# Gated cross-attention with a quantised feed-forward: the batch's row sum moves from TensorE to ScalarE and Pool, W1 is applied to the attended rows, and x is normalised on VectorE

## The reference

```python
h   = layernorm(x)
Sim = (h @ w1)[:, :, None] + (ctx @ w2)[:, None, :] + einsum('bid,bjd->bij', h * w3, ctx) + b_sim
A   = softmax(Sim, axis=2);            hq = einsum('bij,bjd->bid', A, ctx)
Bt  = softmax(max(Sim, axis=2), 1);    hc = einsum('bi,bid->bd', Bt, h)[:, None, :]
x   = x + tanh(g_xattn) * (concat([h, hq, h * hq, h * hc]) @ W_qv + b_qv)
x   = x + tanh(g_ffn) * ffn(layernorm(x))     # 256 -> 768 -> 256, weights and activations quantised
```

## Time and profile before

| | |
|---|---|
| median of 3 runs | 500.15 us (500.15 to 500.7) |
| the profiled execution | 500.24 us, its span 498.0 us |
| attention part | 0 to 224.7 us of the span |
| busy over the span | TensorE 467.1 us (94%), VectorE 347.6 (70%), ScalarE 278.5 (56%), Pool 42.8 (9%) |
| mean granted TensorE clock | 0.983 |

### The profile page before, as it was taken

How to read it: one execution, slowest core, us unless ns; L and a number is a source line. 1 busy time by engine, 2 the same in 40 slices (tenths; PEclk the granted TensorE clock), 3 DMA queues, 4 the chain that set the end, 5 groups by cost and what they waited for, 6 DMA issues and landing times.

```text
span 498.0 us, 6971 instructions
## 1 busy us (share of the span) xinstructions
PE 467.1 (94%) x2542; PEld 306.2 (61%) x2542; DVE 347.6 (70%) x648; ACT 278.5 (56%) x325; POOL 42.8 (9%) x51
## 2 busy tenths in 40 slices
PE   4899999998999979989999999999949999999997
PEld 3787885987488548754444444444414444588886
DVE  6464683687257754769443558999988888898874
ACT  3795241634151200528334379999977677888760
POOL 1111111242013110210000000000100000000000
PEclk9999999998999998999999999999969999999999
DMA  8920000200020020020000000000000000234432
GB/s 246 327 91 1 0 2 12 74 1 1 0 86 0 1 84 2 0 86 0 0 0 0 0 0 0 0 0 1 1 0 0 0 0 0 85 107 128 144 113 103
DMA packets 20671, 21.11 MB, mean 42 GB/s; under 512 B 826, under 2 KB 20393, under 8 KB 20649
## 3 DMA queue, kind: packets, MB, share of 16 engines
q1 hardware_dynamic: 20628, 20.82, 13.2%
q10 hardware_dynamic: 20, 0.00, 0.0%
HBM read 12.43 MB, written 8.39 MB: 42 GB/s over the span
## 4 chain that ended last, share of the span: by engine, by line
PE 56%; issue 17%; DVE 14%; ACT 10%; POOL 1%; DMA 1%; ACTq 0%; POOLq 0%; DVEq 0%
PE ps L672 11%; PE ps L647 10%; PE ps L652 5%; PE ps L495 4%; PE ps L491 4%; PE ps L474 4%; PE ps L499 4%; ACT ag L863 3%; PE ps L537 3%; ACT hid L870 3%; PE ps L454 3%; DVE hid L1279 2%; ACT gq L858 2%; PE ps L440 1%; PE ps L463 1%
## 5 line engine op out<-in xcount | busy, mean ns | idle before, releaser
L647 PE MATMUL ps<-xh,wuh 128*128 128x512 f16 x192 | 73.9, 385 | 9.3 <-DVE gq L1304 7.4
L647 PE MATMUL ps<-xh,wul 128*128 128x512 f16 x192 | 73.8, 384 | 0.0
L652 PE MATMUL ps<-xl,wuh 128*128 128x512 f16 x192 | 58.0, 384 | 0.0
L1251 DVE TENSOR_REDUCE cols<-hid x12 | 27.4, 2286 | 30.5 <-ACT hid L852 30.5
L852 ACT ACTIVATE hid<-ps 128x2048 f32 x12 | 22.5, 1875 | 34.5 <-PE ps L652 34.5
L647 PEld LDWEIGHTS ps<-xh,wuh 128*128 x192 | 19.0, 99 | 34.7 <-issue 11.2
L672 PE MATMUL ps<-wdh,oh 128*128 128x256 f16 x168 | 37.4, 273 | 0.0
L672 PE MATMUL ps<-wdl,oh 128*128 128x256 f16 x168 | 37.4, 273 | 0.0
L647 PE MATMUL ps<-xh,wgh 128*128 128x512 f16 x96 | 36.4, 379 | 0.7 <-DVE xh L1239 0.7
L647 PE MATMUL ps<-xh,wgl 128*128 128x512 f16 x96 | 36.4, 379 | 0.0
L491 PE MATMUL ps<-cw,aT 77*128 77x256 f32 x128 | 35.5, 392 | 0.9 <-ACT cols L801 0.9
(11 more groups left out here) (199 smaller groups left out, 945.9 us busy)
## 6 DMA issues: line engine op xcount, KB each, us to landing
x_scratch<-xa SPq DMA_DIRECT2D x4, 1024.0 KB, 4.4
xo<-x_scratch SPq DMA_DIRECT2D x16, 256.0 KB, 2.7
out_dram<-xo SPq DMA_DIRECT2D x15, 256.0 KB, 2.2
xa<-in_x SPq DMA_DIRECT2D x3, 1024.0 KB, 12.1
xa<-in_x SPq DMA_DIRECT2D x4, 256.0 KB, 4.7
wv<-in_L_xattn_W_qv SPq DMA_DIRECT2D x1, 1024.0 KB, 8.1
wr<-in_L_ffn_w_gate SPq DMA_DIRECT2D x1, 768.0 KB, 9.6
wr<-in_L_ffn_w_up SPq DMA_DIRECT2D x1, 768.0 KB, 11.0
```

The lines of the kernel that those rows point to most:

```text
L647: pe.matmul(ps[hf][:, q, :], w_[:, d, ds(k * P, P)], xh[:, d, n], start=d == 0 and w_ is wh, stop=False)
L652: mm = pe.matmul(ps[hf][:, q, :], wh[:, d, ds(k * P, P)], xl[:, d, n], start=False, stop=d == KD - 1)
L1251: dve.tensor_reduce(gmx[:, ds(k * 2 + hf, 1)], unit(hid, k, hf), AX.X, ALU.max, apply_absolute_value=True).then_inc(gm_done, 1)
```

## The change

What it does, part by part:

- **Attended x W1.** `context_w` and `context_wv` are gone. ScalarE copies `hq_bank` to SBUF (`hqT`), and `project` multiplies `hqT` by W1 itself. VectorE's `attended` reads `hqT` instead of `hq_bank`, so it waits for ScalarE. The bias is multiplied once by tanh(g) (`txb`) and added to `xa` by Pool (`bias_x`).
- **Row sums.** `row_sum` and `row_copy` are gone. ScalarE and Pool each weigh four of the eight row tiles of h in place (`row_weigh`, slot s = 1), and Pool adds them down to one tile (slots s = 1 and 2). `batch_cols` sums that tile over its partitions by a matmul.
- **The batch column one slot later.** `batch_cols` and `summary` move from s = 2 to s = 3, on TensorE right ahead of the `project` that needs `we`.
- **The norm of x** moves from ScalarE to VectorE; `row_shift` is gone.
- **Pool's order**: `y_std`, then `row_weigh` or `row_add`, then `row_std`, `bias_x`, and the weights.

```diff
@@ Pool
+            def row_weigh(b):
+                par = b % 2
+                pool.wait_ge(eb_rdy, b + 1)
+                for t in range(TB // 2, TB):
+                    i_ = pool.tensor_scalar(h[:, par, t, :], h[:, par, t, :], eb[:, t:t + 1], 1.0, ALU.mult, ALU.mult)
+                i_.then_inc(hp_rdy, 1)
+                pool.wait_ge(hp_rdy, b + 1)
+                pool.tensor_tensor(h[:, par, 4:6, :], h[:, par, 4:6, :], h[:, par, 6:8, :], ALU.add).then_inc(hsum_rdy, 1)
+            def row_add(b):
+                par = b % 2
+                pool.wait_ge(ha_rdy, b + 1)
+                pool.tensor_tensor(h[:, par, 0:2, :], h[:, par, 0:2, :], h[:, par, 2:4, :], ALU.add).then_inc(hsum_rdy, 1)
+                pool.wait_ge(hsum_rdy, 3 * b + 2)
+                pool.tensor_tensor(h[:, par, 0:2, :], h[:, par, 0:2, :], h[:, par, 4:6, :], ALU.add).then_inc(hsum_rdy, 1)
+                pool.wait_ge(hsum_rdy, 3 * b + 3)
+                pool.tensor_tensor(h[:, par, 0, :], h[:, par, 0, :], h[:, par, 1, :], ALU.add).then_inc(hs_rdy, 1)
+            def bias_x(n):
+                pool.wait_ge(h_rdy, n + 1)
+                if n == 0:
+                    pool.wait_ge(txb_rdy, 1)
+                x_ = xa[:, 2 * n:2 * n + 2, :]
+                pool.tensor_tensor(x_, x_, txb[:].unsqueeze(1).broadcast_to([P, 2, D]), ALU.add).then_inc(xb_rdy, 1)
...
                 if LAG <= m < L + LAG:
                     y_std(m - LAG)
+                b, s = m // NP, m % NP
+                if s == 1 and 1 <= b <= B:
+                    row_weigh(b - 1)
+                if s == 2 and 1 <= b <= B:
+                    row_add(b - 1)
                 if 1 <= m and m + 3 < N:
                     row_std(m + 3)
+                if s in (0, 3) and 4 <= m < N + 4:
+                    for n in range(2):
+                        bias_x(m - 4 + n if s == 0 else m - 5 + n)
@@ TensorE
             def attend(n):
-                ge(pe, pr_rdy, n)
+                ge(pe, hqT_rdy, n)
...
-            def project(n, summed=None):
+            def project(n):
...
-                    for k in range(2):
-                        pe.matmul(o_, aT[0:JP, par, k, q], cw[0:JP, b % 3, k, :], start=k == 0, stop=False)
-                        if summed is not None:
-                            row_sum(summed, 4 * t + k)
+                    for d in range(KD):
+                        pe.matmul(o_, hqT[:, par, d, q], wv[:, KD + d, :], start=d == 0, stop=False)
...
             def batch_cols(b):
-                pe.wait_ge(hrow_rdy, b + 1)
+                pe.wait_ge(hs_rdy, b + 1)
                 for d in range(KD):
-                    pe.matmul(m_bank[:, HC + d:HC + d + 1], hrow[0:1, d * P:(d + 1) * P], ones[0:1, 0:1], start=True, stop=True)
+                    pe.matmul(m_bank[:, HC + d:HC + d + 1], h[:, b % 2, 0, d * P:(d + 1) * P], ones[:, 0:1], start=True, stop=True)
...
                 if s == 3 and b + 1 < B:
                     context_bias(b + 1)
-                if m == 1:
-                    context_w(0)
-                if s == 0 and 1 <= b < B:
-                    context_w(b)
+                if s == 3 and 1 <= b <= B:
+                    batch_cols(b - 1)
                 if LAG <= m and late:
                     project(m - LAG)
@@ ScalarE
+            def attended(n):
+                act.wait_ge(hq_ps, n + 1)
                 ge(act, f_ps, n - 2 * NP + 1)
+                act.activation(hqT[:, par, :, s * PT:(s + 1) * PT], hq_bank.rearrange("p (d n) -> p d n", d=KD),
+                               ACT.Copy).then_inc(hqT_rdy, 1)
+            def row_weigh(b):
+                act.wait_ge(eb_rdy, b + 1)
+                for t in range(TB // 2):
+                    a_ = act.activation(h[:, b % 2, t, :], h[:, b % 2, t, :], ACT.Copy, scale=eb[:, t:t + 1])
+                a_.then_inc(ha_rdy, 1)
...
-                if m + 1 < N:
-                    norm_x(m + 1)
...
                     normed(m - 1)
                 if s == 1 and b == 1:
                     batch_exp(b - 1)
+                if 3 <= m <= N + 2:
+                    attended(m - 3)
+                if s == 1 and 1 <= b <= B:
+                    row_weigh(b - 1)
@@ VectorE
+            def norm_x(n):
                 dve.wait_ge(rstd_rdy, n + 1)
+                ge(dve, hc_ps, b - 1)
+                for t in range(2 * s, 2 * s + 2):
+                    c = par * TB + t
+                    i_ = dve.tensor_scalar(h[:, par, t, :], xa[:, b * TB + t, :], mv[:, par, t, 0:1], rstd[:, c:c + 1],
+                                           ALU.subtract, ALU.mult)
+                i_.then_inc(h_rdy, 1)
...
             def attended(n):
-                dve.wait_ge(hq_ps, n + 1)
+                dve.wait_ge(hqT_rdy, n + 1)
...
-                dve.tensor_tensor(prT[:, par, :, q], hq_bank.rearrange("p (d n) -> p d n", d=KD), hT[:, par, :, q],
-                                  ALU.mult).then_inc(pr_rdy, 1)
+                dve.tensor_tensor(prT[:, par, :, q], hqT[:, par, :, q], hT[:, par, :, q], ALU.mult).then_inc(pr_rdy, 1)
...
             def residual(n):
                 dve.wait_ge(f_ps, n + 1)
+                dve.wait_ge(xb_rdy, n + 1)
...
                 if m == 0:
-                    row_shift(3)
+                    norm_x(3)
+                if 3 < m and m + 1 < N and s < 3:
+                    norm_x(m + 1)
...
-                if 2 <= m and m + 2 < N:
-                    row_shift(m + 2)
-                if s == 2 and 1 < b <= B:
-                    summary(b - 1)
...
                 if 3 <= m <= N + 2:
                     attended(m - 3)
+                if s == 3 and 1 <= b <= B:
+                    summary(b - 1)
+                if s == 3 and m + 1 < N:
+                    norm_x(m + 1)
                 if LAG <= m and late:
                     residual(m - LAG)
                     norm_x1(m - LAG)
```

More of the change, by code:

```diff
@@ L586, in _ @@
                 if LAG <= m and not late:
-                    project(m - LAG, b - 1 if s == 2 and 1 <= b <= B else None)
+                    project(m - LAG)
                 if s == 1 and 1 <= b <= B and LAG <= m:
@@ L597, in _ @@
                     score(m - 1)
-                if s == 2 and b == 1:
-                    pe.wait_ge(eb_rdy, b)
-                    for t in range(TB):
-                        row_sum(b - 1, t)
                 if 2 <= m <= N + 1:
@@ L605, in _ @@
                     batch_max(b - 1)
-                if s == 2 and 1 < b <= B:
-                    batch_cols(b - 1)
                 if 3 <= m <= N + 2:
                     attend(m - 3)
-                if s == 2 and b == 1:
-                    batch_cols(b - 1)
                 if LAG < m:
@@ L1034, in last_y @@
             def last_y():
+                dve.wait_ge(xb_rdy, N)
                 for t in range(2):
@@ L1145, in _ @@
             stats(1)
-            row_shift(0)
+            norm_x(0)
             dve.wait_ge(bs_rdy, 1)
```

102 lines of the change are left out of this document (30 added, 72 removed).

## The result

The changed kernel takes 515.51 us (median of 4 runs, 514.09 to 516.36) against 500.15: ratio 1.0305, 95% interval 1.0277 to 1.0334. Its profiled execution took 514.09 us, its span 512.3. (Ratios leave out disturbed runs, one of e17's four and five of e18's ten; medians and the bounds beside them don't.) TensorE is busy for 461.2 us (90%), VectorE 366.4 (72%), ScalarE 277.4 (54%), Pool 91.3 (18%); the granted clock is 0.937 where it was 0.983.

A forecast was written before the change was run, and what follows sets the result against it. By time alone TensorE bounds the attention part, but the change lengthens VectorE's in-order waits. Walk -9.9, locks +8 and clock +4.8 sum to +2.9 us on a profiled 500.24 (median 500.15): forecast 503, range 493 to 511.

The forecast's parts named there:

- the slower side: Whole kernel: the chance that the changed kernel is slower, 0.51, against faster 0.36 and same 0.13.
- the walk: VectorE's slots between the starts of project(0), (4), (8), (12): +1.9, -1.7, -5.6, -4.5, sum -9.9 us.
- to project(0): Start up to project(0): VectorE and ScalarE alone form the chain, start moves from 48.17 to 50.0 to 50.1, +1.9 us.
- the lock term: Pool's added SBUF operations holding up VectorE's: 3, 2 and 3 us by stretch, +8; 0 at best, some 15 at worst.
- the price of bias_x: Pool's bias additions, four a batch at 1.05 us each, in front of the next slot's vp2; priced within +8.
- The clock: TensorE stands 4 us before each project(4b), then runs at half clock: three new losses, +4.8 us (0 to 6.4).
- The product, +1.4: VectorE's prT waits for ScalarE's copy, starting 1.5 us after the reciprocal instead of 0.1; nothing can fill it.
- The summary as a dead end: Slots with s = 3: prT, then summary, 1.35 us, and only then may project(4b) start.
- TensorE's loss of 27 us: TensorE's work removed: row sums 20.2 us and context_w 6.9, so its busy time falls by some 27 us.
- The lock rule: A Pool operation on SBUF shuts out some of VectorE's until it ends; prT with two SBUF inputs joins those.
- Pool's queue becomes the bound: Rival: y_std late in each slot 1 and 2 by 1 to 2 us over the forecast, 509 to 516; chance 0.10.
- The chain is relieved: Rival, faster: Pool's locks fall into VectorE's waits and the clock holds at short stands, 496 us; chance 0.31.

The follow-up runs named there:

- e17: Changed kernel with VectorE's product read from PSUM (hq_bank), ScalarE's copy behind it, and without bias_x: 489.02 us, ratio 0.9760.
- e18: Changed kernel with product from PSUM, sums as TensorE column matmuls, column and summary at s = 2, norm of x back on ScalarE: 501.57 us.
- e1: Changed kernel without Pool's 16 bias additions (bias left out of the result): 503.40 us, ratio 1.0064 to the kernel before.
- e3: Changed kernel with VectorE's product read from PSUM again and ScalarE's copy behind it: 500.46 us, ratio 1.0007 to the kernel before.
- e9: Kernel before the change with only batch_cols and summary moved to s = 3: 510.02 us against 500.64, ratio 1.0201.
- e10: Kernel before with batch vector by one-column TensorE matmuls, those of batches 0 to 2 two behind each W1 and W2 matmul: 498.97 us.
- e12: Changed kernel with product from PSUM, sums as TensorE column matmuls spread over attend, column and summary at s = 2, no bias_x: 489.09 us.

## Why the prediction was wrong

It gave the slower side 0.51, so naming the direction was close to a toss; it named the chain, and forecast 503 where 515.5 came: the sum was +2.9, the result +15.4 (+14 against the profiled execution). By its steps, in the profiled execution:

| stretch | forecast by the walk | after | over | e1 (no bias), over |
|---|---|---|---|---|
| to project(0) | 50.1 | 50.1 | 0.0 | +0.2 |
| (0) to (4) | 45.3 | 50.2 | +4.9 | +3.6 |
| (4) to (8) | 45.4 | 53.1 | +7.7 | +4.6 |
| (8) to (12) | 36.7 | 44.6 | +7.9 | +3.4 |
| (12) to the end | 310.7 | 314.2 | +3.5 | +0.7 |
| sum | 488.2 | 512.3 | +24.1 | +12.5 |

Over the walk the forecast booked 12.8 us, 8 for locks and 4.8 for the clock. Without the bias the excess is 12.5. So **the step that failed is the lock term, +8, and in it the price of bias_x**, which took 12.1 us by itself:

- *Its place.* The prediction had it "in front of the next slot's vp2", and gave the place right behind y_std to row_add. At 63.55 it met vp2 and cost it 0.5 us, as that has it. This holds only while row_std stands between y_std and bias_x, and it does so only in slots with m + 3 < N. In the slots 15, 16 and 19 bias_x came right behind y_std, where norm_x1 starts: at 163.57 and 208.07, though Pool had been idle for 16.91 and 10.82 us before y_std, two additions ran back to back and norm_x1 took 2.62 us instead of 0.74; at 172.99 `diag` took 1.40 and norm_x1 1.69. At 115.43 it pushed weight_n back, and this shows a way that the prediction did not price: Pool comes late first, and then VectorE waits for it:
```profile
115.43 2.50 POOL L414 TENSOR_TENSOR xa<-xa,txb 128x512 f32<-128x512 f32 x2
117.90 2.76 POOL L386 TENSOR_TENSOR wr<-wr,wsc 128x1536 f32<-128x1536 f32 x1
120.63 0.69 POOL L367 TENSOR_TENSOR cols<-cols 128x2 f32<-128x2 f32 x1
```
```profile
117.61 0.35 DVE L1033 TENSOR_SCALAR cols<-cols 128x2 f32<-128x2 f32 x1
...
118.66 2.09 DVE L1075 TENSOR_SCALAR diag<-ident,cols 128x128 f32<-128x128 f32 x1
```

  vp2 was there at 117.96, y_std started at 120.63, and `diag` took 2.09 us instead of 0.29. Not all of this is the bias: weight_n holds this slot in the other kernels too, at vp2. From the start of residual to that of norm_x1 it is 5.59 us here, 4.45 in e1 and 5.09 before. norm_x1 took over 2.2 us five times in all, two of them against bias_x and three against row_add.
- *Its length.* 512 columns were interpolated at 1.05 us; they took 1.27 (weighing one tile took 0.478, near the 0.45 taken).
- *Its sum.* "As the nearest row shows a full hit, I take 3 us ..., 2 ..., and 3": 8 us for 16 additions of bias, 16 weighings and 16 additions of rows. Removing the bias alone gave 12.1 us, more than the whole term; removing the sums alone gave 9.0. Less the clock (below, 6.9 to 10.4), 14 to 17 of the 24.1 us are left for this term, about the 15 that I had called every one in full.
- *What a hit costs.* 8.4 us on VectorE came with 12 us of time. A hit lengthens TensorE's stand too, and the half clock after it. The prediction added locks and clock as if one didn't feed the other.

**The clock**: +4.8 was taken for three new stands of 1.6. project(0), (4), (8) and (12) took 7.1, 8.3, 7.3 and 7.2 us instead of 5.3, 8.5 too much in all (29.9 - 4 x 5.35), of which before paid 1.6 at project(12): 6.9 new. The attends before project(4) and (8), 3.66 and 3.62 us instead of 1.89, were at half clock too, 3.5 more. Filling the stands gave back 7.4, though project(0) itself then starts 2.4 us later and project(12) stays at half clock. The term was short by at least 2.1. Its picture was off as well: no stand of 4 us lies before project(4) and (8), but one of 3.04 and 1.95 us at the scores and a second of 1.48, and the clock was down before the second began.

**After project(12)** the walk had no change, and that was wrong by 3.5 us. Without the bias it is 0.7: again bias_x, whose pairs reach 209 us.

**What held.** To project(0): 50.14, forecast 50.1; 5.98 us of it are the exchange, as e3 starts at 44.16, where five products by the walk's 1.4 are 7, so that this stretch came out to 0.1 us is in part luck. The product, +1.4 forecast, waits in 14 of 16 slots, mostly 1.28 us. The summary as a dead end ahead of project(4b) is shown by e9: 9.4 us for its later place alone, a dead end that the walk had counted, though not at a price of its own. TensorE's loss of 27 us did not show as busy time (467.1 to 461.2), as many of its matmuls ran at half clock; in e17, at a clock of 0.965, it is 445.4, 21.7 less than before.

**The lock rule.** Rows 8 and 9 gave it and e1 to e3 confirm it. In the kernel after, the product that began at 81.03, with both inputs in SBUF, took 1.17 us beside Pool's addition of 80.38 to 81.65; in e3 the one at 127.59, with an input in PSUM, took 0.67 beside Pool's operation of 127.41 to 128.93. All 16 of e3 stayed within 664 to 692 ns, residual within its 0.75. The Trainium skill, "SBUF — State Buffer", section "Who interferes with whom", says that an instruction of VectorE with two inputs in SBUF contends with one of GpSimd that reads SBUF, and that the one that issues first keeps the shared ports for its whole instruction; the trace agrees, by the product above and by norm_x1, which ended at 166.26 where Pool's pair ended at 166.11. What was missing was the list, slot by slot, of what VectorE wants when Pool starts. The Trainium skill, "GPSIMD Engine Reference", section "Engine selection", calls one-input work of GpSimd roughly line rate, and the prediction estimated from it weighings at my lower bound, 0.3 us; they took 0.478 (median), so the 2 us that this would have saved did not come.

**The rivals.** "Pool's queue becomes the bound" named 509 to 516, and the time fell into it, but not by its mechanism: y_std started within 0.8 us of vp2 in 13 of 15 cases; once vp2 itself was held for 2.63 us, and once, as shown above, y_std was 2.7 us late, never by a slot. That share of the rival did happen; it isn't most of the loss. "The chain is relieved", 496, needed locks and clock under 8.9; together they were some 24 over the walk. With sums, late column and norm kept, the kernel was faster than before only without bias_x and exchange (e17, 489.02).

## What to carry to other kernels

Work moved from the bound engine to an idle one costs what its *start* meets: put a Pool operation on SBUF where VectorE reads PSUM or waits, never right behind the small result that VectorE is waiting for. Before shifting an operand from PSUM to an SBUF copy, keep the consumer on PSUM and let the copy run behind it: same work, 15 us here. And price a summary by the slot it stands in; one slot later, with all else alike, cost 9 us in two kernels and 3.7 in a third.

## What the runs showed that was not expected

- TensorE fell to half clock without standing: 4.41 us of one-column matmuls (32 records), and the next attend took 3.76 us instead of 1.89, at a granted clock of 0.50. In e10, with four such records behind every two of 256 columns, the same work left attend at 1.97 and the clock of its stretch at 1.00. In e12, with eight behind every two, the stretch read 0.92.
- Two prices on one chain, 11.4 and 14.4, added up to within 0.7 us of their joint 26.5, and yet no price was a property of its part. Taken out of the kernel after (or of one near it) and put into e12, in which TensorE is busy nearly throughout, the same part costs differently: exchange 14.4 and 4.1, late column 9.1 and 3.7, bias 11.4 and 7.5.
- Records of a one-row, 256-column float32 matmul were no shorter than those of 128 rows (435 ns in the mean, 415 for those of W1 beside them).
